# Local attention layers: row norm split between the attention loop on GpSimd and the gated layer

## What is computed

```python
h = shift_token(x)                       # second half of the features comes from the token before
q, k, v = split(h @ wqkv); q, k = rotary_xpos(l2norm(q) * qs, l2norm(k) * ksc)
x = x + local_attention(q, k, v) @ wo    # 8 heads of 64, windows of 64 tokens
h = shift_token(x)
h = (h - mean(h)) / sqrt(var(h) + 1e-5) * lg + lb
a, g = split(h @ w1 + b1)                # 341 features each
x = x + (a * gelu(g)) @ w2 + b2
```

## Time and profile before

| | us |
|---|---|
| median of 3 runs | 2612.56 (2603.31 to 2613.4) |
| the profiled execution, its own time | 2607.94 |
| its span | 2606.2 |
| busy PE / DVE / ACT / POOL | 2169.4 / 1882.0 / 1510.9 / 742.8 |

### The profile page before, as it was taken

One profiled execution on the slowest core, in us unless ns is written; L12 is line 12 of the kernel. 1 busy time (PEld: TensorE's weight loads), 2 busy tenths in 40 slices (PEclk: granted clock), 3 DMA queues, 4 the chain that ended last, 5 costly groups with the idle time before them and its releaser, 6 DMA issues. The chain is left out here.

```text
span 2606.2 us, 57526 instructions
## 1 busy us (share of the span) xinstructions
PE 2169.4 (83%) x22021; PEld 1134.5 (44%) x22050; DVE 1882.0 (72%) x2884; ACT 1510.9 (58%) x3177; POOL 742.8 (28%) x1323
## 2 busy tenths in 40 slices
PE   5998567699999999966866999999688888876688
PEld 2663334133333333225753444444347546655533
DVE  5556765999999999825457778786486596657577
ACT  2563553288888888852432777777468357542321
POOL 3780000000000000002740122222296386504356
PEclk8997777699999999986976999999899998987789
DMA  3220001511212112001123222221101010010000
GB/s 93 77 66 3 12 1 62 112 41 41 55 28 55 46 36 55 3 4 31 51 51 100 65 68 69 68 68 30 42 23 31 9 38 6 20 25 3 1 1 17
DMA packets 79725, 104.66 MB, mean 40 GB/s; under 512 B 35287, under 2 KB 53881, under 8 KB 79454
## 3 DMA queue, kind: packets, MB, share of 16 engines
q1 hardware_dynamic: 67102, 90.22, 13.2%
q10 hardware_dynamic: 9856, 5.64, 1.1%
q0 software_dynamic: 2496, 5.12, 0.7%
HBM read 80.53 MB, written 14.09 MB: 36 GB/s over the span
## 5 line engine op out<-in xcount | busy, mean ns | idle before, releaser
L978 DVE TENSOR_REDUCE l1a_core_mpart<-l1a_core_psA 128x1 f32<-128x1024 f32 x512 | 600.9, 1219 | 39.2 <-PE l1a_core_psA L890 27.7
L960 ACT ACTIVATE l1a_core_prob<-l1a_core_psB 128x512 f32<-128x512 f32 x1024 | 551.9, 596 | 101.2 <-PE l1a_core_psB L905 87.8
L1322 ACT ACTIVATE l2a_core_prob<-l2a_core_psB 128x384 f32<-128x384 f32 (+3 forms) x656 | 303.6, 526 | 133.6 <-PE l2a_core_psB L1260 129.8
L1347 DVE TENSOR_REDUCE l2a_core_mpart<-l2a_core_psA 128x1 f32<-128x1024 f32 (+4 forms) x352 | 291.1, 879 | 40.5 <-PE l2a_core_psA L1242 38.8
L917 PE MATMUL l1a_core_psV<-l1a_core_prob,l1a_core_vh 128*32 128x512 f32 x2048 | 266.5, 596 | 0.2 <-ACT l1a_core_prob L960 0.2
L905 PE MATMUL l1a_core_psB<-l1a_core_qh,l1a_core_kh 75*32 75x512 bf16 x2560 | 196.2, 383 | 0.5 <-ACT l1a_core_prob L960 0.5
L1276 PE MATMUL l2a_core_psV<-l2a_core_prob,l2a_core_vh 128*32 128x256 f32 (+3 forms) x1856 | 168.0, 419 | 0.4
L1187 POOL TENSOR_SCALAR_AFFINE_SELECT l2a_core_prob<-l2a_core_prob 128x128 f32<-128x128 f32 x256 | 73.9, 293 | 314.4 <-ACT l2a_core_prob L1322 310.8
L850 POOL CAST l1a_core_mb<-l1a_core_negm 128x16 bf16<-128x16 f32 x16 | 3.1, 196 | 472.4 <-PE l1a_core_psA L890 408.4
L1260 PE MATMUL l2a_core_psB<-l2a_core_qh,l2a_core_kh 75*32 75x512 bf16 (+3 forms) x1720 | 134.8, 338 | 0.9 <-ACT l2a_core_prob L1322 0.7
L905 PE MATMUL l1a_core_psB<-l1a_first_qh,l1a_first_kh 75*32 75x512 bf16 x1536 | 119.2, 387 | 4.8 <-ACT l1a_core_prob L960 4.8
(11 more groups left out here) (740 smaller groups left out, 4570.4 us busy)
## 6 DMA issues: line engine op xcount, KB each, us to landing
l2f_tab<-in_rotary SPq DMA_DIRECT2D x32, 128.0 KB, 2.1
l0a_core_qh<-qparts SPq DMA_DIRECT2D x36, 96.0 KB
l0a_core_kh<-kparts SPq DMA_DIRECT2D x36, 96.0 KB
l1a_core_qa<-qparts SPq DMA_DIRECT2D x32, 96.0 KB
l1a_core_ka<-kparts SPq DMA_DIRECT2D x32, 96.0 KB
l2a_core_qa<-qparts SPq DMA_DIRECT2D x32, 96.0 KB
l2a_core_ka<-kparts SPq DMA_DIRECT2D x32, 96.0 KB
l1a_core_qh<-qparts SPq DMA_DIRECT2D x30, 96.0 KB
```

What stands on the lines that cost most here:

```text
L960: nc.scalar.activation(prob[u % (2 * PER_KB)][:], psB[u % 3][:], ACT.Exp, scale=scale).then_inc(b_exped, 1)
L978: nc.vector.tensor_reduce(mpart[:, n // 2, n % 2:n % 2 + 1], psA[i % 2][:], AX.X, ALU.max).then_inc(a_freed, 1)
L1322: nc.scalar.activation(prob[n % RING][:, 0:cols], psB[n % 3][:, 0:cols], ACT.Exp, scale=scale).then_inc(b_exped, 1)
L1347: ins = nc.vector.tensor_reduce(mpart[:, place, part:part + 1], psA[i % 2][:, lo * P:hi * P], AX.X, ALU.max)
```

## The change

- In the attention loop DVE takes the moments of chunks 0 and 1 at the end of steps 9 and 13. POOL does their `power` and their `normalise` behind its copies of rows 10 and 14. `normalise` has `nc.gpsimd.tensor_scalar` for those chunks, each of the four waiting for the one before, and `nc.vector.tensor_scalar` for chunks 2 and 3.
- Chunk 3's transfers move to the head of SP's list in `local_ffn`. Chunks 2 and 3 get moments behind units 0 and 1 and normalise behind units 1 and 2, all on DVE; POOL's `power` for both comes first there, and its bias additions wait until all 16 rows are normalised.
- PE's order begins turn(0), inputs(0), turn(1) and ends down(3), turn(6), turn(7). ACT begins with a Gelu of one element.
- In the second layer the last chunk of the next norm takes ACT's Sqrt and DVE's reciprocal instead of POOL's `power`.

```diff
+    def normalise_by_root(self, dve, c):
+        dve.wait_ge(self.std_ready, c + 1)
+        self.nc.vector.reciprocal(self.rstd[:, 4 * c:4 * c + 4], self.std[:, 4 * c:4 * c + 4]).then_inc(self.rstd_ready, 1)
+        self.normalise_by_power(dve, c)
...
-    def normalise(self, dve, c):
...
+    def normalise(self, eng, c):
+        rows, scale = self.rows, self.nc.gpsimd.tensor_scalar if c < NC - 2 else self.nc.vector.tensor_scalar
+        eng.wait_ge(self.rstd_ready, c + 1)
         for t in range(4 * c, 4 * c + 4):
+            if c < NC - 2 and t % 4:
+                eng.wait_ge(self.normed, t)
+            scale(rows[:, t, :], rows[:, t, :], self.mv[:, t, 0:1], self.rstd[:, t:t + 1],
...
-            for c in range(NC):
+            for c in range(NC - 1):
                 sp.wait_ge(added, 4 * (c + 1))
                 shifted.shift(sp, c)
...
-            pool.wait_ge(back_ready, 2 * NT)
-            for c in range(NC - 1):
-                shifted.power(pool, c)
+                if t in (10, 14):
+                    pool.wait_ge(back_ready, 2 * (t + 1))
+                    shifted.power(pool, (t - 10) // 4)
+                    shifted.normalise(pool, (t - 10) // 4)
+                    pool.wait_ge(shifted.normed, t - 6)
...
-                if 0 <= n - NT < NC - 1:
-                    shifted.moments(dve, n - NT)
-                if 0 < n - NT < NC:
-                    shifted.normalise(dve, n - NT - 1)
+                if n in (9, 13):
+                    shifted.moments(dve, (n - 9) // 4)
...
+        @block.sync
+        def _(sp):
+            shifted.shift(sp, NC - 1)
+            if on_sync is not None:
                 on_sync(sp)
...
             pool.wait_ge(loaded, W * (l + 1))
+            shifted.power(pool, NC - 2)
+            shifted.power(pool, NC - 1)
+            pool.wait_ge(shifted.normed, NT)
...
-                if c == 0:
-                    shifted.power(pool, NC - 1)
-            for c in range(NC if norm else 0):
+            for c in range(NC - 1 if norm else 0):
                 norm.power(pool, c)
...
             turn(0)
-            turn(1)
...
-                    if k == 0 and 1 <= c < NC - 1:
+                    if k == 0 and c < NC - 1:
                         turn(c + 1)
...
+            down(NC - 1)
             turn(2 * NC - 2)
-            down(NC - 1)
             turn(2 * NC - 1)
...
+            nc.scalar.activation(first[:], g.ident[0:1, 0:1], ACT.Gelu)
             out(0)
-            out(1)
...
+            if norm:
+                norm.root(act, NC - 1, NC)
             out_next(NC - 2)
...
-                if c == 0 and k == 1:
-                    shifted.moments(dve, NC - 1)
-                if c == 0 and k == 2:
-                    shifted.normalise(dve, NC - 1)
+                if n < 2:
+                    shifted.moments(dve, NC - 2 + n)
+                if 1 <= n < 3:
+                    shifted.normalise(dve, NC - 3 + n)
...
             if norm:
-                norm.normalise_by_power(dve, NC - 1)
+                norm.normalise_by_root(dve, NC - 1)
```

More of the change, by code:

```diff
@@ L3709, in power @@
         self.nc.gpsimd.tensor_tensor(r, r, self.g.minus_half[:], ALU.pow).then_inc(self.rstd_ready, 1)
-    def normalise(self, dve, c):
-        nc, rows = self.nc, self.rows
-        dve.wait_ge(self.rstd_ready, c + 1)
+    def normalise(self, eng, c):
+        rows, scale = self.rows, self.nc.gpsimd.tensor_scalar if c < NC - 2 else self.nc.vector.tensor_scalar
+        eng.wait_ge(self.rstd_ready, c + 1)
         for t in range(4 * c, 4 * c + 4):
-            nc.vector.tensor_scalar(rows[:, t, :], rows[:, t, :], self.mv[:, t, 0:1], self.rstd[:, t:t + 1],
+            if c < NC - 2 and t % 4:
+                eng.wait_ge(self.normed, t)
+            scale(rows[:, t, :], rows[:, t, :], self.mv[:, t, 0:1], self.rstd[:, t:t + 1],
                                     ALU.subtract, ALU.mult).then_inc(self.normed, 1)
@@ L4061, in local_ffn @@
     h = [st.sb(f"h{i}", [P, 3, CH]) for i in range(2)]
+    first = st.sb("first", [1, 1])
     psA = [st.ps(f"psA{i}") for i in range(2)]
@@ L4075, in local_ffn @@
     with st.block() as block:
-        if on_sync is not None:
-            @block.sync
-            def _(sp):
+        @block.sync
+        def _(sp):
+            shifted.shift(sp, NC - 1)
+            if on_sync is not None:
                 on_sync(sp)
```

## The result

The changed kernel takes **2620.85 us** (median of 16 runs, 2613.91 to 2629.18) beside 2611.80 of the kernel before in as many runs: a ratio of 1.0026, with a 95% interval of 1.0014 to 1.0039. It is slower by 4 to 10 us where I had forecast 10 faster than the median then shown, and the time lies 10 us above the top of my range. By the bound of 0.5% it is no change; by the interval it is a small loss.

What follows compares the result with a forecast made beforehand. It took the attention loop to be a chain without slack through GpSimd's multiplication, the gated layer to be TensorE's. Gains of 14.6 us less 9.1 lost gave net 5.5, from 2607.94 to 2602 us, range 2592 to 2611.

Steps and rivals of the forecast that it cites:

- the price T: Attention loop: length of one GpSimd normalise instruction, taken as 0.40 us; insertion 1.90 + 4T, four insertions lose 9.1 us.
- rival (b): Attention loop: GpSimd's normalise is dear; loss 4 x (0.68 + 4T) eats the whole gain from T = 0.74 on; chance 0.10.
- The clock at the gated layers' start: With TensorE's gap cut to about 0.7 us the clock stays up: 0.85 us a layer, 1.7 gained.
- No recovery and no slack in the loop: Attention loop: beyond GpSimd's 1.22 us of idle time, each insertion's delay of 2.28 us reaches the end.
- rival (a): The attention loop takes up GpSimd's work: loss only 0 to 2 us, kernel at 2593 to 2595; chance 0.16.
- The moments at no cost: Attention steps 9 and 13: VectorE's moments, 1.10 us, fit its 1.09 us of idle time; at most 0.1 each.
- The start: Start of the gated layer: TensorE's block begins 4.3 us earlier in each layer, 8.6 gained in all.
- rival (c): Gated layer's start doesn't follow SP, or the clock still falls: 3 to 5 us of gain missing; chance 0.08.
- the 1.2 that I gave as a sign: Gated layer's start: its first transposes should come about 1.2 us behind the last projection in the profile after.
- The table load on the path: Gated layer's start: ACT's 1.28 us load delays first inputs to 2.43 us after the block, from 2.10; 0.7 lost in both layers.
- The tail: End of the second gated layer: the last normalise starts near 2300.4 instead of 2306.06, 5.7 us gained.
- The first layer's end: First gated layer: VectorE's upper copy ahead of the last addition gives the gain back; nothing, within 1 us either way.

Runs made afterwards that it cites:

- e4: The changed kernel with 17 and 22 unread matmuls on TensorE ahead of the transposes of rows 11 and 15; 2615.99 us, 0.9998 of the kernel before.
- e1: The changed kernel with chunks 0 and 1's power behind GpSimd's last copies and their normalise on VectorE in steps 17 and 18; 2598.40 us, 0.994 of before.
- e5: e1 without the one-element Gelu at the head of ACT's list; 2597.55 us, 0.9925 of the kernel before.
- e2: As e1, but GpSimd's power stays in the loop behind the copies of rows 10 and 14; 2600.55 us, 0.9937 of the kernel before.
- e7: e5 with the gated layer's last addition ahead of the upper copy on VectorE; 2593.84 us, 0.9902 of the kernel before.
- e3: The changed kernel with GpSimd's normalise as two tensor_tensor instructions of 128x512 per chunk instead of four tensor_scalar; 2612.87 us, 0.999 of the kernel before.
- e9: e2 with five further GpSimd tensor_scalar instructions into scratch behind its two powers, for their durations alone; 2610.44 us in one run.
- e6: The kernel before with the change's tail alone: last down product earlier, Sqrt and reciprocal for the second layer's last chunk; 2610.15 us, 0.9968 of before.

## Why the prediction was wrong

**The step that failed is the price T in the cost of the loop.** I bounded it by 0.29 and 0.73 and took 0.40, "one tensor is read, as in the first, with two operations on it". It is 0.796, above my upper bound: the product of two tensors twice as wide is no upper bound for `tensor_scalar`, which is slower per column. The mechanism around it was right: 1.90 + 4T is 5.08 us with the measured T, and 5.17 were seen; 4 x (0.68 + 4T) is 15.5, and e4 shows 15.2. With the right T the sum would have been 14.6 - 15.5, no change: 2608.8 us, inside the range. This was rival (b), to which I gave 0.10, and the place, T above 0.74, was the one it named.

**A second term was missing: the clock in the loop.** I looked at the clock only at the gated layer's start, although there too TensorE's wait came first. With T = 0.796 it waits 3.93 us in the insertion of row 10 and 5.23 in that of row 14, does nothing, and its next work runs at half speed. That cost 6.6 to 8.5 us, shown by e4, and turned no change into a loss. Rival (b) left it out as well. Between the 5.5 us gained that I forecast and the 9.05 lost lie 14.6 us: some 6.1 are T (15.2 lost instead of 9.1), 6.6 to 8.5 this term, 1.7 the next one. The forecast also started from an execution of 2607.94 us, 3.9 below the median of the 16 runs.

**The clock at the gated layers' start** did not stay up in the changed kernel, so the 1.7 us weren't gained; it did in e1 and e5. The term was too small as well: e1's two gated layers are 3.37 us shorter than the changed kernel's. e1 and e2 differ only in where `power` stands, 0.4 to 0.5 us of the loop, and it stayed up in the one and fell in the other; e4 has both in one run. Why stays open.

**What was right.** No recovery and no slack in the loop (rival (a) falls): in e4 the steps of the insertions take 8.41 to 8.47 us and those between them 4.52. The moments at no cost (e1). The start: 4.26 and 4.32 us of idle time gone where 4.3 a layer was predicted (rival (c) falls but for the clock). TensorE's transposes come 0.65 us behind the last projection; the sum had 0.66, and the 1.2 that I gave as a sign didn't agree with it. The table load on the path: inputs start 2.26 us after the block where I had 2.43; e5 puts its price at 0.62 a layer, and shows that it could have been had for nothing. The tail: 5.9 us where 5.7 was predicted. The first layer's end: nothing, for the reason given (e7).

**Open: the projections between the layers.** They took 84.12 and 84.18 us in the changed kernel's two profiles and 78.78 before, but 81.9 in e3 and 81.8 in e4, which have the change's loop, 80.1 in e1, 81.3 in e2, 82.9 in e5, 81.2 in e7 and 84.29 in e9, which haven't the norm in it, and 80.9 in e6, where nothing ahead of them but one product's order is changed. In those of 82.9 and more VectorE's small scalings take 0.79 to 0.83 us in the mean, in the others 0.63 to 0.66, but 0.84 in e7, whose projections aren't long; so they don't explain it. The medians don't need these 5 us, the profiled executions hold them, and no experiment ties them to the change.

## What to carry to other kernels

In this loop GpSimd, which idled 1.22 us a step, took that much more work for nothing and passed on nearly all the rest; the same norm fits for nothing where VectorE waits for the last products. Before work is moved to GpSimd, have a row of that very instruction: one of another operation on a similar shape bounds nothing. And when a delay makes TensorE wait, count work at half speed behind the wait as part of the delay: here waits of 3.9 and 5.2 us each brought it, and in e3 one of 2.65 us did in the second layer where one of 2.70 in the first didn't.

## What was unexpected of the hardware

GpSimd's `tensor_scalar` took 0.66 and 1.08 us on 128 and 256 columns with two constants, so some 0.24 us and 3.3 ns for each column, and 0.14 us more with two per-row operands. Four tiles of the norm take 3.2 us that way and 2.1 us as two instructions of 128x512 with a broadcast operand (1.04 each), which are even shorter than the additions of b2 on the same shape (1.27 in both kernels). VectorE's four took 1.12.
